# Decoder block on one core: GpSimd's addition of the output bias, split in two and placed two heads and one head earlier

## What is computed

```
scores  = softmax(q k^T / 4)                       # 512 x 512 per batch and head
keep the 460 columns with the largest column sums  # per batch and head
out     = (scores with the other columns zero) v
x       = layernorm(x + concat(out) @ Wo.T + bo)
```

## Time and profile before

| | us |
|---|---|
| runs | 1951.5, 1948.04, 1950.86 (median 1950.86) |
| the profiled execution | 1951.64 |
| its span | 1949.8 |
| TensorE busy | 1782.1 (91%) |
| VectorE busy | 1263.1 (65%) |
| ScalarE busy | 991.4 (51%) |
| GpSimd busy | 639.8 (33%) |

### The profile page before, as it was taken

The page is one execution under the profiler, slowest core; times in us unless marked ns, Lnnn a source line. Parts: engine busy times, 40 slices in busy tenths (PEclk is TensorE's granted clock), DMA queues, the critical chain, the costliest instruction groups (busy, mean ns, idle before and its releaser), DMA issues. The chain is left out here.

```text
span 1949.8 us, 26129 instructions
## 1 busy us (share of the span) xinstructions
PE 1782.1 (91%) x8373; PEld 1056.6 (54%) x8373; DVE 1263.1 (65%) x2933; ACT 991.4 (51%) x2603; POOL 639.8 (33%) x813
## 2 busy tenths in 40 slices
PE   7999878899898898888879999999689999999997
PEld 5556534455444454444445665565465666566553
DVE  2686568888989999898512211221566878786665
ACT  4336699989989898997321111111242333233220
POOL 2000055555667666666410001000542323222100
PEclk9999989999999999999999999999788999999999
DMA  6247741112212222221763335332411111200000
GB/s 216 81 176 270 258 101 51 54 55 71 82 55 82 79 79 63 85 82 45 252 210 108 108 112 166 121 108 68 138 60 60 47 47 49 49 11 17 11 12 22
DMA packets 164071, 183.29 MB, mean 94 GB/s; under 512 B 19652, under 2 KB 143803, under 8 KB 162912
## 3 DMA queue, kind: packets, MB, share of 16 engines
q1 hardware_dynamic: 157792, 165.46, 26.6%
q0 software_dynamic: 6144, 16.18, 2.7%
HBM read 119.01 MB, written 63.18 MB: 93 GB/s over the span
## 5 line engine op out<-in xcount | busy, mean ns | idle before, releaser
L914 POOL TENSOR_SCALAR xa_probs<-xa_probs,xa_small 128x512 f32<-128x512 f32 x512 | 344.9, 690 | 244.3 <-DVE xa_small L1076 244.3
L985 ACT ACTIVATE xa_probs<-xa_ps_s,xa_small 128x512 f32<-128x512 f32 x512 | 361.0, 743 | 40.2 <-DVE xa_small L1082 36.3
L1082 DVE TENSOR_REDUCE xa_small<-xa_ps_s 128x2 f32<-128x1024 f32 x256 | 309.2, 1208 | 36.9 <-PE xa_ps_s L1353 36.9
L1366 PE MATMUL xa_ps_t<-xa_ident,xa_probs 128*128 128x128 f32 x2048 | 308.5, 283 | 17.4 <-DVE early L744 7.0
L1366 PEld LDWEIGHTS xa_ps_t<-xa_ident,xa_probs 128*128 128x128 f32 x2048 | 229.0, 142 | 153.3 <-ACT early L746 46.4
L2458 PE MATMUL ta_ps_e<-late,ta_x5T 128*128 128x512 f32 x512 | 235.8, 594 | 1.4 <-DVE ta_acc L2211 1.4
L1353 PE MATMUL xa_ps_s<-xa_k,xa_q 96*128 96x512 bf16 x496 | 151.5, 387 | 54.1 <-ACT xa_probs L985 54.1
L1622 ACT ACTIVATE ex_hid<-ex_ps_g 128x512 f32<-128x512 f32 x64 | 38.2, 597 | 270.3 <-PE ex_ps_u L1721 270.2
L2211 DVE SCALAR_TENSOR_TENSOR ta_acc<-ta_ps_e,ta_gate,ta_acc 128x256 f32<-128x256 f32 x256 | 123.6, 483 | 67.0 <-PE ta_ps_e L2458 60.8
L1677 DVE TENSOR_TENSOR ex_hid<-ex_hid,ex_ps_u 128x512 f32<-128x512 f32 x64 | 44.0, 688 | 181.8 <-ACT ex_hid L1622 181.8
L2458 PEld LDWEIGHTS ta_ps_e<-late,ta_x5T 128*128 128x128 f32 x512 | 93.9, 189 | 96.8 <-issue 83.3
(11 more groups left out here) (371 smaller groups left out, 3044.0 us busy)
## 6 DMA issues: line engine op xcount, KB each, us to landing
scratch_qk_parts<-front_w_all SPq DMA_DIRECT2D x16, 768.0 KB, 5.7
xa_q<-scratch_qk_parts SPq DMA_DIRECT2D x186, 64.0 KB
xa_k<-scratch_qk_parts SPq DMA_DIRECT2D x186, 64.0 KB
scratch_buf<-late SPq DMA_DIRECT2D x8, 1024.0 KB, 5.3
early<-in_L_ffn_Wg SPq DMA_DIRECT2D x16, 512.0 KB, 6.0
early<-in_L_ffn_Wu SPq DMA_DIRECT2D x16, 512.0 KB, 6.3
early<-in_L_ffn_Wd SPq DMA_DIRECT2D x16, 512.0 KB, 6.7
ex_xs<-scratch_buf SPq DMA_DIRECT2D x16, 512.0 KB, 5.3
```

Source lines behind the costliest of these rows:

```text
L914: ins = pool.tensor_scalar(probs[n % NP][:, t, :], probs[n % NP][:, t, :], rinv[n % 2][:, t:t + 1], 1.0, ALU.mult, ALU.mult)
L985: ins = act.activation(probs[n % NP][:, t, :], ps_s[j][:, t % 2, :], ACT.Exp, bias=nmax[n % 2][:, t:t + 1], accum_out=rsum[n % 2][:, t:t + 1])
L1082: dve.tensor_reduce(nmax[n % 2][:, 2 * j:2 * j + 2], ps_s[j][:, :, :], AX.X, ALU.max, negate=True).then_inc(max_up, 1)
L1366: ins = pe.transpose(ps_t[t % 2][:, i * P:(i + 1) * P], probs[m % NP][:, i, t * P:(t + 1) * P], ident[:, :])
```

## The change

add_bias takes an index i and adds the bias to two of the four row tiles. Its two calls stand behind normalize in heads h = 3 and h = 4 of unit 1, in place of one call in head h = 5. The wait for the loaded rows is in front of the first. VectorE's add of half i waits for xb_up of its own half. After the loop both calls stand one behind the other.

```diff
-            def add_bias(b):
-                if b == 0:
+            def add_bias(b, i):
+                if (b, i) == (0, 0):
                     pool.wait_ge(c_ld, 48)
-                pool.wait_ge(x_ld[b % 2], 16 * (b // 2 + 1))
-                x = x_in[b % 2]
-                pool.tensor_tensor(x[:, :, :], x[:, :, :], row(bo[:, :]).to_broadcast([P, T, D]), ALU.add).then_inc(xb_up, 1)
+                if i == 0:
+                    pool.wait_ge(x_ld[b % 2], 16 * (b // 2 + 1))
+                x = x_in[b % 2][:, 2 * i:2 * i + 2, :]
+                pool.tensor_tensor(x, x, row(bo[:, :]).to_broadcast([P, 2, D]), ALU.add).then_inc(xb_up, 1)
...
-                if b >= 1 and (u, h) == (1, 5):
-                    add_bias(b - 1)
+                if b >= 1 and u == 1 and h in (3, 4):
+                    add_bias(b - 1, h - 3)
...
-            add_bias(B - 1)
+            add_bias(B - 1, 0)
+            add_bias(B - 1, 1)
...
-                dve.wait_ge(xb_up, b + 1)
+                dve.wait_ge(xb_up, 2 * b + i + 1)
```

## The result

The changed kernel took 1939.49 us (median of 6 runs, 1934.91 to 1940.2), the kernel before, on the same chip, 1951.18 (6 runs, 1948.04 to 1955.03). The ratio is 0.9935, with a 95% interval of 0.9922 to 0.9948: faster by 10.1 to 15.2 us, 11.7 by the medians. The prediction was 1936.5, faster by 14.4. The profiled execution took 1936.2 us, with a span of 1934.4, 15.4 less than before.

What follows compares the result with a forecast made beforehand. TensorE, VectorE and ScalarE together were taken as the bound, held by GpSimd's late bias addition. Seven places at 2.06 us gave 14.4 gained, 0 given back: 1936.5 us, range 1931 to 1944.

Steps and rivals of the forecast that it cites:

- The bound and the releaser: Middle of attention: TensorE, VectorE and ScalarE bound it together; GpSimd's late bias addition alone ends VectorE's wait of 2.14 us.
- The gain at a place: At VectorE's first add in seven batches: 2.06 us gained each, 14.4 us in all.
- the later at the masks: TensorE, reaching the masks at 570.48, was taken to set the gain; VectorE's second add allowed them from 570.40.
- four named waits: TensorE's waits at second output product 0.25, scores 0.70, turning 0.21 and masks 0.90 us: 2.06 us, all to go.
- the walk: Instruction-by-instruction retiming of one place with the bias long done: VectorE 2.14, ScalarE 2.03, TensorE 2.06 us earlier.
- the upper end: Most the change could gain: VectorE's whole wait for the bias addition, 15.0 us over seven places.
- The halves: GpSimd's two additions in heads 3 and 4: about 1.3 us each, fitting idle time and costing nothing.
- The second cover: Behind GpSimd's 0.40 us idle in head 3, TensorE turns that tile later: another 0.4 us of delay free.
- The wait for the loaded rows: Moved from head 5 to head 3 on GpSimd; a landing up to 1.7 us later at the tightest place is free.
- VectorE beside the halves: Search and maxima beside GpSimd's halves in heads 3 and 4: priced at nothing, upper bound 1.3 us for each of 14.
- The sum: Whole kernel: 14.4 us gained, 0 given back; profiled execution 1951.64 to 1937.2, median predicted 1936.5.
- rival 4: Clock after 990 us: the earlier stage may meet other low stretches, 5 us either way, 1931.5 to 1941.5; chance 0.15.

Runs made afterwards that it cites:

- the second experiment: Kernel before, with the whole, unsplit bias addition moved from head h = 5 to h = 4: 1944.72 us, ratio 0.9937.
- the third: Changed kernel, with both halves put back in the old place behind normalizing in head h = 5: 1949.64 us, ratio 0.9964.
- the whole addition: Kernel before, with the whole, unsplit bias addition moved two heads earlier, from h = 5 to h = 3: 1942.74 us, ratio 0.9934.
- the second comparison: Changed kernel timed again without edit, 5 runs against 9 of the kernel before (1955.99 us): 1942.39 us, ratio 0.9932.
- the first comparison: Changed kernel against the kernel before, 6 runs each: 1939.49 against 1951.18 us, ratio 0.9935.

## Why the prediction was right, and by how much it was off

*The bound and the releaser* were right. GpSimd's addition alone ended the wait: moved by one head and otherwise untouched (the second experiment), it sets free all three engines, and with half of the wait left half of the gain is left (the third).

*The gain at a place* was mis-sized: 2.06 us predicted, 2.23 measured, 15.6 in place of 14.4 in all. The step that failed is the one that took TensorE to be the later at the masks (570.48 against 570.40), with only its four named waits gone. In the changed kernel TensorE waits 0.54 us for the second add there, so VectorE sets the pace. Without that wait TensorE would have reached the masks 8.68 us after the first output product, 2.78 earlier than before: it had 0.7 us more to give than the four waits that the trace names, most of it behind the second output product, where two groups of transposes became one run. Then the gain is VectorE's, which the walk put at 2.14 and which measured 2.23. The bound of 15.0 that I had called the upper end was too low for a small reason: on VectorE the next row starts some 0.07 us before the end of the one ahead (MAX8 at 554.20 for 0.68, the add at 554.81), so the wait, read from row end to row start, left this out, and from the add to the maxima it is 0.59 us in place of 0.61.

*The halves*: 1.27 to 1.31 us predicted, 1.27 measured. Head 3 has 0.48 us to spare where I had 0.40. The second cover, TensorE's own turn, had its 0.4 us. What my price left out is the slack behind it: I took each wait of TensorE as lost. The 0.16 us of the whole addition cost nothing, and 2.1 us cost 1.1 to 1.8 where the clock stayed up.

*The wait for the loaded rows* did not come back: no trace has a DMA wait on the addition inside the loop, with the halves in head 3 or with the whole.

*VectorE beside the halves*: nothing was longer, as priced. But that is luck of the place as much as of the kind of instruction. I had weighed MAX8, MATCH_REPLACE8 and the maxima, and not L1096, the one step of the search that runs SBUF to SBUF in 0.41 us; three heads later it is held for 0.36 to 0.60 us.
The Trainium skill (SBUF — State Buffer, Who interferes with whom) has the rule of one port pair under an exclusive lock, which a tensor_scalar of VectorE can need; the 1.01 and 0.77 us rows agree. It names no exception for a GpSimd instruction with a single input, and the 0.63 us row of L1109 and the 0.78 us row of L1150 agree with that too.

*The sum*: 14.4 predicted, 11.7 and 13.6 measured by the medians of the two comparisons. The mechanism gives 15.6. The rest, 2.0 us in the second comparison, goes with the clock, which is rival 4, small. Over all timed runs that list a clock, a least-squares line with one level for each kernel in each comparison and a common slope gives 0.80 us less (standard error 0.06) for each 0.001 more of mean granted clock. The 22 runs of the kernel before that list it had 0.9725 on average, the 25 of the kernels with steps of 5.0 that were timed in rounds 0.9698. That is 2.7 x 0.8 = 2.2 us. At an equal clock of 0.970 the same fit puts the kernel before at 1958.0 and the changed one, on the same chip, at 1941.7, 16.3 us apart. For the first comparison this cannot be done, since the timed runs of the kernel before list no clock there; that 14.4 came as near as it did to 11.7 is in part luck, since the gain at a place was taken too small and the clock was taken to give nothing back. The traces place the extra low stretches behind the loop: from its last reciprocal to the first ex_out copy it is 124.3 and 126.5 us in the two traces of the kernel before, and 125.5 and 127.0 in the changed kernel's two, at mean clocks of 0.96, 0.96, 0.95 and 0.96. In the ten other traces it is 125.3 to 131.5, at 0.91 to 0.95. The kernel with the first half three times over is among them with 130.8, and its loop is as long as that of the kernel before (665.1 us), so a shorter loop alone is not the reason. What is, or whether it is chance, no run here settles.

## What to carry to other kernels

Where the engines of a pipeline are within a few per cent of each other, look for an instruction of a fourth, mostly idle engine that comes due late in a step: its wait was passed on to all of them one for one, and moving it one step ahead, without making it smaller, gave everything back. Check how much idle time the new place has, and then what runs beside it there, instruction by instruction. Measure such a gain by the steps of the loop in the trace (here to 0.01 us) and not by the total alone, where the clock moved single runs by more than 5 us.

## What the runs showed of the hardware that was not expected

- GpSimd's addition of two SBUF inputs held VectorE's SBUF-to-SBUF tensor_scalar: 1.01 and 0.77 us in place of 0.41, ending 0.28 us behind GpSimd's instruction both times. GpSimd's tensor_scalar, with one input, held it too: 0.63 in place of 0.41, and 0.74 to 0.78 in place of 0.40 for L1150. The profile shows no wait for it, only a longer row. MAX8 and MATCH_REPLACE8, and the maxima out of PSUM, were not held.
- Behind a wait of TensorE of 2.1 us the granted clock was at the 1.2 GHz level for 3.4 us at four of seven places that are otherwise alike, and the step there was 1.3 to 1.6 us longer.
- The same addition on 128x512 took 1.27 us with the bias broadcast over the row tiles, in place, and 1.04 us with both inputs the same tensor.
